# Attention with a gated low-rank branch on one core: another order for the moves of q and k, for the splits of the weights, and for the end

## The reference, cut to what matters

```python
xn = layernorm(x)                                    # x: 2 x 512 x 512
q, k = rmsnorm(xn @ Wq.T), rmsnorm(xn @ Wk.T)         # 32 query heads of 128, 8 key heads
v = xn @ Wv.T                                         # 4 query heads share a key head
scores = q @ k.T / sqrt(128) + slope * (j - i)        # causal: -1e30 where j > i
s = (softmax(scores) @ v) @ Wo.T
g = silu(2 * sum_over_8_experts(router * (xn @ A.T) @ B.T))
y = x + s * g
```

## Time and profile before

| | |
|---|---|
| device time, median of 3 runs | 757.17 us (757.09 to 758.48) |
| the profiled execution's own time | 757.56 us |
| its span, first to last instruction | 755.4 us |
| mean granted TensorE clock | 0.994 of 2.4 GHz |
| busy: PE, DVE, ACT, POOL | 95%, 79%, 74%, 48% |
| HBM read and written | 86.17 MB and 62.19 MB |

### The profile page before, as it was taken

How to read it: one execution, slowest core, us unless ns; L and a number is a source line. 1 busy time by engine, 2 the same in 40 slices (tenths; PEclk the granted TensorE clock), 3 DMA queues, 4 the chain that set the end, 5 groups by cost and what they waited for, 6 DMA issues and landing times.

```text
span 755.4 us, 14576 instructions
## 1 busy us (share of the span) xinstructions
PE 720.2 (95%) x3736; PEld 609.3 (81%) x3736; DVE 596.5 (79%) x1468; ACT 562.5 (74%) x1440; POOL 363.9 (48%) x343
## 2 busy tenths in 40 slices
PE   7998999999999999999999999999999999999795
PEld 7787888878888788888888788888888788887665
DVE  6858798778977798678987789687987789777774
ACT  4567787788777788686877887777876877878672
POOL 4225354446444653464534653644544554436256
PEclk9999999999999999999999999999999999999999
DMA  8015969678786868687695777768686786867632
GB/s 298 1 29 151 291 165 260 172 209 231 193 257 159 236 177 243 194 233 222 165 282 146 218 219 216 228 174 258 162 251 173 216 237 181 262 158 194 196 130 83
DMA packets 215877, 148.68 MB, mean 197 GB/s; under 512 B 49072, under 2 KB 206640, under 8 KB 215728
## 3 DMA queue, kind: packets, MB, share of 16 engines
q1 hardware_dynamic: 180720, 128.43, 58.4%
q10 hardware_dynamic: 35136, 20.00, 10.6%
HBM read 86.17 MB, written 62.19 MB: 196 GB/s over the span
## 4 chain that ended last, share of the span: by engine, by line
PE 44%; issue 16%; DVE 13%; ACT 9%; POOL 7%; DMA 4%; SPq 3%; ACTq 2%; DVEq 0%; POOLq 0%
PE qkv_ps L1271 4%; PE qkv_ps L1272 4%; PE qkv_ps L1273 4%; PE out_ps L1271 4%; PE out_ps L1273 4%; PE out_ps L1272 4%; DMA qk_moved<-turning_qk 3%; ACT probs L672 3%; SPq L444 3%; PE score_ps L1271 3%; PE score_ps L1273 2%; PE mix_ps L1271 2%; PE score_ps L1272 2%; PE mix_ps L1273 2%; PE mix_ps L1272 2%
## 5 line engine op out<-in xcount | busy, mean ns | idle before, releaser
L546 POOL TENSOR_TENSOR pt_lo<-x_sb,pt_hi 128x512 fp32r<-128x512 f32 x137 | 174.5, 1298 | 263.3 <-ACT pt_hi L734 263.3
L664 ACT ACTIVATE probs<-probs,neg_max 128x128 f32<-128x128 f32 (+3 forms) x256 | 142.0, 559 | 47.2 <-DVE neg_max L954 46.5
L954 DVE CUSTOM_DVE_ANT_0 probs<-score_ps,cst,slope 128x128 f32<-128x128 f32 (+3 forms) x256 | 129.5, 546 | 33.8 <-PE score_ps L1273 25.2
L672 ACT ACTIVATE probs<-probs,recip 128x128 f32<-128x128 f32 (+3 forms) x252 | 126.3, 549 | 8.2 <-DVE recip L961 8.2
L1271 PE MATMUL qkv_ps<-w_hi,xt_hi 128*128 128x256 f32 (+1 forms) x392 | 126.4, 322 | 2.4 <-DVE xt_lo L897 1.4
L1272 PE MATMUL qkv_ps<-w_lo,xt_hi 128*128 128x256 f32 (+1 forms) x392 | 126.4, 322 | 0.0
L1273 PE MATMUL qkv_ps<-w_hi,xt_lo 128*128 128x256 f32 (+1 forms) x392 | 126.0, 321 | 0.0
L1271 PE MATMUL out_ps<-wo_hi,o_hi 128*128 128x512 f32 x252 | 101.6, 403 | 3.3 <-DVE o_lo L998 3.3
L536 POOL TENSOR_TENSOR inv_rms<-sums,minus_half 128x5 f32<-128x5 f32 x64 | 78.6, 1228 | 52.9 <-DVE sums L1012 52.8
L975 DVE STREAM_TRANSPOSE squared<-probs 128x256 f32<-128x256 f32 (+3 forms) x124 | 101.8, 823 | 1.2 <-ACT probs L672 0.3
L1273 PE MATMUL out_ps<-wo_hi,o_lo 128*128 128x512 f32 x252 | 99.8, 396 | 0.0
(11 more groups left out here) (172 smaller groups left out, 1626.1 us busy)
## 6 DMA issues: line engine op xcount, KB each, us to landing
turning_qk<-qk_squared ACTq DMA_DIRECT2D x244, 80.0 KB, 2.0
qk_moved<-turning_qk SPq DMA_DIRECT2D x61, 320.0 KB, 3.4
turning<-squared SPq DMA_DIRECT2D x120, 128.0 KB, 2.4
x_sb<-turning SPq DMA_DIRECT2D x30, 512.0 KB, 5.1
w_raw<-wqkv SPq DMA_DIRECT2D x32, 384.0 KB, 5.2
turning<-squared SPq DMA_DIRECT2D x120, 96.0 KB, 2.0
x_sb<-turning SPq DMA_DIRECT2D x30, 384.0 KB, 4.2
turning<-squared SPq DMA_DIRECT2D x128, 64.0 KB, 1.8
```

The lines of the kernel that those rows point to most:

```text
L546: nc.gpsimd.tensor_tensor(by_quad(pt_lo, j), moved_block(t, j), by_quad(pt_hi, j).bitcast(F32), ALU.subtract).then_inc(pt_lo_by_pool, 1)
L664: nc.scalar.activation(probs[:, h, 0:n], probs[:, h, 0:n], ACT.Exp, bias=neg_max[:, h:h + 1], scale=-1.0, accum_out=total[:, h:h + 1]).the ...
L672: nc.scalar.activation(to[:, h, 0:n], probs[:, h, 0:n], ACT.Copy, scale=recip[:, h:h + 1]).then_inc(probs_ready, 1)
L954: nc.vector.tensor_tensor_reduce(probs[:, h, 0:n], score_bank(t, h), cst[:, C_DIST + SEQ - n:C_DIST + SEQ], slope[:, h:h + 1], HUGE, ALU.a ...
```

## The change

- **SP.** `move` is split up. In every slot from 2 on, SP writes the first pair of probabilities, then waits until the former q and k are used up and the next ones written, reads these, and only then writes the second pair.
- **ACT.** `mixed_hi` comes before `write_qk` (except in slot 10).
- **DVE.** `mixed_lo` moves: in slots whose next block is narrow it comes before the second `square_probs`; otherwise it comes in the following slot, behind the first head's `bias`. DVE makes three of the four `w_lo`, and one of the four `wo_lo` (head 2).
- **POOL.** It makes one `w_lo` and three `wo_lo`; it waits for DVE's `turned_qk_lo` before it splits the probabilities.
- **PE.** The scores of blocks 0 and 4 no longer wait for `k_lo`, which they do not use.
- **The end.** q and k of the last block are turned by PE (five transposes) into PSUM and split into `w_hi` and `w_lo`, in place of the way over HBM; the fourth head's scores of blocks 6 and 7, the gates and the splits stand elsewhere; POOL finishes y of block 0 in slot 4 and of block 1 in slot 5, and blocks 2 to 5 ahead of `start_last_y`; x is read again later.

```diff
-            def move(g, t, u):
+            def move(g, t, u, soon=False):
...
+                write_probs(g, t, 0)
+                if soon and u is not None:
+                    sp.wait_ge(qk_lo_ready, K_AND_Q_LO(g, u, 0))
+                    read_qk(g, u)
+                write_probs(g, t, 1)
...
+            def read_qk(g, u):
+                sp.wait_ge(qk_written, QK_WRITTEN(g, u - BY_TURN, 16 * QUADS))
+                sp.dma_start(qk_moved[:, :, :], turning_qk[u % 2, :, :, :].rearrange("q p n -> p q n")).then_inc(qk_moved_ready, 16)
...
             def slot(g, t, left):
-                if t % BLOCKS == W_SLOT:
+                if t % BLOCKS == W_SLOT and here(t + 3, left):
                     turned_lo(g, t - 2)
                 if here(t + 2, left):
                     inverse_rms(g, t + 2)
                 if t % BLOCKS == W_SLOT and here(t + 3, left):
-                    split_w(g + 1, range(EARLY_W, KC))
+                    split_w(g + 1, range(W_DVE, KC))
+                elif t % BLOCKS == W_SLOT:
+
+                    turned_lo(g, t - 2)
...
+                if left == 1 and t == 4:
+                    finish_y(0)
                 if here(t - 1, left) and not by_both(t - 1):
+
+                    pool.wait_ge(qk_lo_ready, K_AND_Q_LO(g, t + 2, 0))
+                    if left == 1 and t == W_SLOT:
+                        finish_y(1)
                     turned_lo(g, t - 1)
...
             def end(g):
                 turned_lo(g, BY_PE - 1)
-                pool.wait_ge(x_again, 16 * BLOCKS)
-                for m in range(4):
+                for m in range(2, BLOCKS - 2):
                     finish_y(m)
                 start_last_y()
-                for m in range(4, BLOCKS - 2):
-                    finish_y(m)
...
-                if here(t + 2, left):
+                if wo_due:
                     write_qk(g, t + 2)
-                if wo_due:
                     act.wait_ge(out_ready, ONE(g, t - 2, 0))
                     split_wo(g + t // BLOCKS, range(0, HPG))
                 if here(t - 2, left):
                     mixed_hi(g, t - 2, left)
+                if by_squares(t + 2, left) and not wo_due:
+                    write_qk(g, t + 2)
...
                 if here(t, left):
                     bias(g, t, 0)
+                if here(t - 3, left) and wide(t):
+                    mixed_lo(g, t - 3, left)
+                if here(t, left):
                     bias(g, t, 1)
...
                 if here(t + 1, left):
                     turned_qk_lo(g, t + 1)
+                if here(t - 2, left) and not wide(t + 1):
+                    mixed_lo(g, t - 2, left)
                 if here(t, left):
                     square_probs(g, t, 2)
-                if here(t - 2, left):
-                    mixed_lo(g, t - 2, left)
-                if left == 1 and t == 4:
-                    multiply_gate(range(2, 4))
+                if t % BLOCKS == 2 and here(t, left) and t > 2:
+                    split_wo(g + t // BLOCKS)
...
-                if h == 0:
+                if h == 0 and (t % QB > 0 or t == 0):
                     pe.wait_ge(qk_lo_ready, K_AND_Q_LO(g, t + 1, 0))
-                    if t % QB == 0:
-                        pe.wait_ge(k_full_ready, PER_BATCH(g, t, 1))
+                if h == 0 and t % QB == 0:
+                    pe.wait_ge(k_full_ready, PER_BATCH(g, t, 1))
...
+            def turn_last_qk(g, u):
+
+                pe.wait_ge(q_norm_ready, ONE(g, u, 1))
+                pe.wait_ge(k_norm_ready, ONE(g, u, 1))
+                for h in range(HPG):
+                    tr = pe.transpose(turn_ps[:, h * P:(h + 1) * P], qk_norm[:, h, :], ident)
+                tr.then_inc(qk_turned, 1)
+                pe.transpose(qkv_ps[:, 0, 0:P], qk_norm[:, HPG, :], ident).then_inc(qk_turned, 1)
```

More of the change, by code:

```diff
@@ L216, in build @@
         x_late += [wo_raw[:, m, :] for m in range(2)]
-        gate_tanh = [wo_raw[:, 2 + m % 2, :] for m in range(BLOCKS)]
+        gate_tanh = [wo_raw[:, (m + 2) % 4, :] for m in range(BLOCKS - 2)]
+        gate_tanh += [part[:, :, :].rearrange("p a n -> p (a n)")[:, 0:DM] for part in (qk_squared, qk_moved)]
         qkv_ps = psum("qkv_ps", [2, 512])
@@ L248, in build @@
         wo_loaded = sem("wo_loaded")
-        x_again = sem("x_again")
+        x_again = [sem(f"x_again{k}") for k in range(BLOCKS // 2)]
         stored = sem("stored")
@@ L384, in has_half, with by_squares, is_last @@
             return t >= 2 and keys_of(t) <= 2
+        def by_squares(t, left):
+            return here(t, left) and not is_last(t, left)
+        def is_last(t, left):
+            return left == 1 and t == BLOCKS - 1
         def last_turns(t):
@@ L431, in _ @@
             sp.dma_start(wo_raw[:, :, :].rearrange("p c n -> p (c n)"), wo[0:1].rearrange("a p n -> p (a n)")).then_inc(wo_loaded, 16)
-            def move(g, t, u):
+            def move(g, t, u, soon=False):
                 i, to = t % QB, moved[t % 2]
                 n = (i + 1) * P // 2
[L441 to L448, removed]
+                write_probs(g, t, 0)
[3 more added lines that the diff above has]
+                write_probs(g, t, 1)
+                if u is not None and not soon:
+                    read_qk(g, u)
                 for pair in range(2):
@@ L465, in slot @@
             def slot(g, t, left):
+                if left == 1 and t == 3:
+                    load_x_again(range(0, 2))
                 if left > 1 and t in (3, 4):
@@ L760, in slot @@
                     normalize_probs(g, t, range(0, 2))
-                if left == 1 and t < W_SLOT:
-                    gate_tangents(range(2 * (t - 3), 2 * (t - 3) + 2))
+                if left == 1 and t == 3:
+                    gate_tangents(range(0, 2))
+                if left == 1 and t == 4:
+                    gate_tangents(range(2, 6))
                 if here(t + 1, left) and not (left == 1 and t == W_SLOT):
@@ L778, in end @@
                 before, last = BLOCKS - 2, BLOCKS - 1
-                exponentials(g, before, range(0, HPG))
-                turned_qk_hi(g, last)
+                turned_qk_hi(g, last, True)
+                exponentials(g, before, range(0, 3))
                 for pair in range(2):
@@ L785, in end @@
                 mixed_hi(g, before - 2, 1)
+                exponentials(g, before, range(3, HPG))
                 normalize_probs(g, before, range(2, HPG), late_probs)
                 moved_hi(g, before - 1)
-                gate_tangents(range(4, 6))
-                exponentials(g, last, range(0, 3))
+                gate_tangents(range(6, BLOCKS))
+                exponentials(g, last, range(0, 2))
                 mixed_hi(g, before - 1, 1)
@@ L939, in set_factor, with bias @@
                 nc.vector.tensor_copy(factor[:, :], cst[:, bass.ds(col + C_FACTOR, NORMED)]).then_inc(factor_set, 1)
-            def bias(g, t, h, at_end=False):
+            def bias(g, t, h, at_end=False, singly=False):
                 n = keys_of(t) * P
-                by_twos = t > 2 and not at_end and (h >= 2 or has_half(t))
+                by_twos = t > 2 and not at_end and not singly and (h >= 2 or has_half(t))
                 if not (by_twos and h % 2 == 1):
@@ L1411, in scores @@
                 else:
-                    last = three(out, q_hi[:, hs], q_lo[:, hs], k_hi[:, b, 0:n], k_lo[:, b, 0:n], True, True)
+                    last = three(out, q[0][:, hs], q[1][:, hs], k_hi[:, b, 0:n], k_lo[:, b, 0:n], True, True)
                 last.then_inc(scores_ready, 1)
@@ L1505, in end @@
                 before, last = BLOCKS - 2, BLOCKS - 1
-                for h in range(HPG):
+                for h in range(3):
                     scores(g, before, h)
+                turn_last_qk(g, last)
                 out(g, before - 3)
+                scores(g, before, 3)
                 mix(g, before - 2, 1)
                 for h in range(3):
-                    scores(g, last, h)
+                    scores(g, last, h, last_q)
                 out(g, before - 2)
+                scores(g, last, 3, last_q)
                 mix(g, before - 1, 1)
@@ L1515, in end @@
                     turn_probs(before, n)
-                scores(g, last, 3)
                 out(g, before - 1)
```

166 lines of the change are left out of this document (107 added, 59 removed).

## The result

The changed kernel takes 778.27 us (median of 4 runs, 773.73 to 780.22) where the kernel before takes 757.13 (4 runs): a ratio of 1.0254, with a 95% interval of 1.0214 to 1.0295. It is 21 us slower where 13 us faster had been forecast. The profiled execution of the changed kernel took 780.22 us, 2 us above its median, with a span of 778.4 us.

The account below looks back on a forecast made before the run. PE, busy 720.2 of 755.4 us, was taken as the bound, so only its waits could be won. Loop 6.6 plus end 6.8 gave 13.4 us, forecast 743.8 us; own range 739 to 749, wider range 736 to 752.

Parts of the forecast that it names:

- The rival with SP: Slots 3 and 7: SP held, second pair late, PE loses up to 1.3 us per wide block; 760.5 us, chance 0.05.
- by the row of block 7's `pt_hi`, which waited for nothing, most of it has slack: Block 7's `pt_hi` began at 396.38 with no wait shown, so most of the second pair's delay was taken as harmless.
- `k_lo` of slot 10 and its 1.04 us of slack: Before slot 10's scores: `k_lo` ends 1.04 us ahead, which a late chain can use up before PE notices.
- 14.9 us: Within the slower case: the gain of the rest of the sum, without its 1.5 us for new waits.
- another order wins no bandwidth: Shared DMA engines: the probabilities pay in full for the earlier read, the sum losing 7 x 2 x 1.0 us.
- the earlier reads do nothing: ACT's `q_hi` may wait for q and k where ACT has time; the sum holds no gain from the reads.
- The loop's 6.6 us: Gain forecast for the loop: 7.6 from small waits, plus 0.5 in slot 5, less 1.5 for new waits.
- the second rival: Loop: PE arrives earlier but the next slot's chain holds it, so only the end wins; 750.4 us, chance 0.17.
- The waits of slots 3 and 4: PE's waits for the bias, `o_lo` and `k_lo`, 8.9 us in seven passes, six sevenths (7.6 us) counted as won.
- The part of it that I forecast for slot 5: `q_lo` falls from 1.52 to 0.65 us, paying for a third `w_lo`; the wait changes name, 0.5 of 2.9 won.
- The end: Block 7's q and k by PE transposes: 5.9 us won, less 1.5 for late `o_lo`; with the tail, 6.8 us.
- The tail: After the last matmul: block 5's y no longer holds SP, the last store is issued sooner; 2.4 us won.

Follow-up runs that it names:

- c3: The changed kernel with the early read of q and k in slots 3 and 7 of each pass alone; 772.46 us, ratio 1.0217.
- a1: The changed kernel with SP's old order, q and k read behind both pairs of probabilities; 750.08 us, ratio 0.9892.
- b4: The changed kernel with the early read in narrow slots (0 and 1 of four) only, SP's old order in wide ones; 746.55 us, ratio 0.9837.
- b2: The changed kernel with SP's old order and two `w_lo` each on DVE and POOL; 747.95 us, ratio 0.9858.
- c1: The changed kernel with early reads in narrow slots only and two `w_lo` each on DVE and POOL; 746.34 us, ratio 0.986.

## Why the prediction was wrong

**The rival with SP was the case, and the prediction had set it aside.** The prediction named the place (slots 3 and 7), the mechanism (320 KB go ahead of the second pair, which comes about 1 us later) and the price (up to 1.3 us for each wide block, slower from 2.1 us a pass). It gave this a chance of 0.05. Measured in c3 against a1: 630.8 - 610.2 = 20.6 us in seven passes, 2.9 us a pass. The step that failed is "by the row of block 7's `pt_hi`, which waited for nothing, most of it has slack". A row without a wait shows only that the data had come, not by how much. Another pass of the same trace of before had this:

```profile
309.62 1.16 ACT L734 ACTIVATE pt_hi<-x_sb 128x512 fp32r<-128x512 f32 x2 [0.47 <-DMA x_sb<-turning]
```

There the read-back landed 0.47 us after ACT was ready for it, and in one other pass 0.29 us after (at 268.00): in these passes ACT had no slack. In the others the rows do not say how much there was. The size of the delay was low as well: 1.0 us had been worked out for the second pair, and the second read-back in slot 3 of c3 goes out 7.85 - 6.10 = 1.75 us later.

The second error was the path. The prediction let the delay go through `k_lo` of slot 10 and its 1.04 us of slack; it went through `pt_hi` and `pt_lo` into `mix` of the same block, where less absorbs it. Part of the price was mis-attributed too: the wait for ACT's writes, from which the rival took its name, is worth 3 us.

Even the rival's own time, 760.5 us, is 18 us too low. It let the rest of the change win 14.9 us, where 7 were won (a1), and it counted 18.2 us for slots 3 and 7, where 22 were lost. Reading early in all slots costs some 6 us beyond that; no run shows where these arise.

The Trainium skill (DMA: Bandwidth & Descriptors, "Issuing engines are not separate DMA queues") says that DMAs interleave on the same 16 DMA engines whoever starts them. What q and k won on ACT (36 us of waiting) and the probabilities lost (37 us) fits such sharing. But SP starts both of these moves, so no run here tests DMAs that different engines start; and that another order wins no bandwidth was the prediction's inference, not the page's words.

**Whether the earlier reads do nothing in narrow slots stays open.** There the next read-back has time. From a1 to b4 the time goes from 750.08 to 746.55 us, and the two intervals overlap only at 0.9863 to 0.9867. But with two `w_lo` each the same step (b2 to c1) leaves the ratio where it was, 0.9858 and 0.986, and of the 4.1 us between the spans of a1 and b4 only 1.1 lie in the seven passes. A gain of a few us is likely, but not shown. Why there should be one is only argued: `o_lo` ahead of the second pair (DVE's new order) makes the old read of q and k later, and the early one mends that.

**The loop's 6.6 us: the second rival.** Without the early read the kernel takes 750.08 us, where "the loop's waits only move" gave 750.4. The waits of slots 3 and 4 did go as forecast, and slot 5 took the time back. In one pass, from the `mix` of slot 3 to that of block 3, before took 358.52 - 337.58 = 20.94 us, and a1 359.28 - 339.22 = 20.06; to the first scores of slot 6 it was 366.30 - 337.58 = 28.72, and now 28.47; the mean of the first six passes is 28.6 and 28.7. The rows of a1 that stand between:

```profile
364.22 1.85 POOL L553 TENSOR_TENSOR w_lo<-w_raw,w_hi 128x768 fp32r<-128x768 f32 x1 [2.26 <-DVE w_lo L1099]
...
366.13 0.50 PE L1355 MATMUL turn_ps<-w_hi,xt_hi 128*128 128x512 f32 x1 [0.57 <-POOL w_lo L553]
...
367.69 0.44 PE L1355 MATMUL score_ps<-k_hi,q_hi 128*128 128x384 f32 x1 [0.25 <-DVE k_lo L1046]
```

PE comes 0.9 us sooner to a slot in which it had already been waiting, and most of that is gone by the scores. In the six passes together, PE's waits in this stretch grow from 2.6 us, all of it for `w_lo`, to 5.2: 3.2 for `w_lo`, which comes through ACT, DVE and POOL, 1.5 for `k_lo` and 0.5 for `pt_lo`. The growth, 0.43 us a pass, is half of what slot 5 takes back, some 0.86 us a pass; the other half stands in no row of a wait. The step that failed here is adding up the waits of slots 3 and 4 as won, although the next wait of the same pass stood behind work that PE doesn't start. The part of it that I forecast for slot 5 held in its sizes: `q_lo` fell from 1.52 us to 0.65 with POOL out of its way, and the wait for `k_lo` appeared. In the trace of before, this instruction takes 1.51 to 1.53 us in slot 5 of every pass and about 0.65 elsewhere; in a1 it takes 0.65 to 0.69 everywhere. The Trainium skill (SBUF — State Buffer, "Who interferes with whom") says that a DVE instruction with two inputs in SBUF contends with a GpSimd instruction that reads SBUF, through ports that the two share; these durations agree with it. What bounds the loop in the end, which of the engines on these chains has to become faster, stays open: no run made the seven passes shorter than 606 us.

**The end was right in its parts.** From the `mix` of block 3 to PE's end the changed kernel wins 42.4 - 37.7 = 4.7 us, a1 3.3 and b4 5.1, forecast 5.9 - 1.5 = 4.4. Block 7's scores start 748.07 - 741.27 = 6.8 us after block 6's, where before it was 722.88 - 710.20 = 12.7: 5.9 us sooner, as forecast. The clock no longer falls there, and DVE's gates hold `o_lo` as said: PE waits 1.79 and 0.50 us for it, in place of the 1.5 us that had been taken from between 0 and 3.2. The changed kernel's windows (length, busy of PE, PEld, DVE, ACT, POOL, PEclk, DMA share, GB/s) and rows:

```profile
742.00:759.00 17.00, 14.88 (x71) 11.34 (x69) 15.22 (x34) 13.63 (x32) 9.34 (x8) 1.00 0.61 192
759.00:775.00 16.00, 15.46 (x97) 13.69 (x97) 11.49 (x18) 6.32 (x13) 13.10 (x10) 1.00 0.20 76
```

```profile
755.12 3.27 DVE L1123 SCALAR_TENSOR_TENSOR gate<-wo_raw,gate 128x512 f32<-128x512 f32 x2
...
759.04 0.50 PE L1355 MATMUL out_ps<-wo_hi,o_hi 128*128 128x512 f32 x1 [1.79 <-DVE o_lo L1054]
...
775.50 1.13 SPq L532 DMA_DIRECT2D y<-acc  x2
775.84 0.43 DVE L1138 TENSOR_TENSOR acc<-acc,wo_raw 128x256 f32<-128x256 f32 x1
```

The tail wins 6.8 - 3.2 = 3.6 us instead of 2.4: not only is SP free, but DVE's last step takes 0.43 us, against 1.03 beside a busy POOL.

## What to carry to other kernels

- That an instruction waits for nothing in one pass is no measure of its slack, the time by which its input could come later without harm. Before a transfer is put ahead of another on the same DMA engines, look at all passes for how soon the consumer of the other one starts after it lands, and take the slack as zero where any pass shows a wait.
- An earlier read is a trade between two consumers. Here it costs nothing in slots whose probabilities have time, and 22 us in the two slots of eight whose probabilities are awaited. The choice by slot (746.6 us) beats both kernels, but most of that gain is there without any early read (a1, 750.1).
- Waits that are small and follow one another in a loop can't be added up. What is won at one place counts only as far as the next place at which the engine already waits for a chain that it doesn't start itself.

## What the runs showed of the hardware

After the waits of 1.24 and 0.72 us at 375.60 and 377.28 in the changed kernel the granted clock fell to the lower of its two levels for some 3.5 us, and then rose again (windows as above):

```profile
375.60:377.28 1.68, 0.96 (x3) 0.48 (x3) 1.68 (x2) 1.61 (x3) 1.68 (x2) 1.00 0.03 7
377.28:380.80 3.52, 3.52 (x8) 2.79 (x9) 3.27 (x7) 3.52 (x12) 2.21 (x2) 0.52 0.71 168
380.80:384.00 3.20, 3.20 (x19) 2.75 (x18) 3.17 (x6) 2.93 (x8) 1.86 (x1) 1.00 0.29 66
```

Matmuls of 512 columns start 0.43 us apart in the middle window (378.25, 378.68, 379.10) and 0.23 us apart in the last (381.03, 381.27, 381.50). Three more such stretches lie in the seven passes of this trace, from 101.76 to about 107.7, from 558 to 562 and from 650 to 654. Each follows a wait for `pt_lo`, of 2.81 us or of 1.52 and 0.72, or 1.36 and 0.73 us. As PE works at about half its rate for some 17 us in all, they are worth about 8 of the loop's 26.7 us (an estimate from the granted clock of each us). In the profile this time counts as busy. It is part of why PE's "busy" time rose from 720.2 to 737.8 us with five matmuls more. Not every wait has this after it: behind the wait of 1.79 us at 759.04 the granted clock is 1.00.
